# Feed-forward stage of an attention block: the second layer's first group of products ahead of the next block's projection

## The reference

```
y  = attention(x)                       # [4096, 1024]
x1 = layernorm(x + y @ Wproj)
h  = silu(x1 @ w1.T * s1) * (x1 @ w2.T * s2)      # layer one, 256 -> 1024
h  = gelu(h @ h1.T * s_h1)                        # layer two, 1024 -> 1024
h  = gelu(h @ h2.T * s_h2)                        # layer three
out = layernorm(x1 + h @ w3.T * s3)
```

## Time and profile before

| what | us |
|---|---|
| median of 3 runs | 3362.25 |
| lowest and highest run | 3346.83, 3367.85 |
| profiled execution, time | 3363.94 |
| profiled execution, span | 3362.1 |
| TensorE busy in the span | 3158.6 (94%) |
| mean granted clock of TensorE | 0.975 |

### The profile page before, as it was taken

One profiled execution on the slowest core, in us unless ns is written; L12 is line 12 of the kernel. 1 busy time (PEld: TensorE's weight loads), 2 busy tenths in 40 slices (PEclk: granted clock), 3 DMA queues, 4 the chain that ended last, 5 costly groups with the idle time before them and its releaser, 6 DMA issues. The chain is left out here.

```text
span 3362.1 us, 45968 instructions
## 1 busy us (share of the span) xinstructions
PE 3158.6 (94%) x15472; PEld 2462.0 (73%) x15472; DVE 1671.5 (50%) x3928; ACT 1792.8 (53%) x3057; POOL 1491.0 (44%) x1306
## 2 busy tenths in 40 slices
PE   3899999999999999999999999989999999999998
PEld 3667767667667677676676776678888888788887
DVE  6566566565565655665655656442222322232322
ACT  2477677676666766776766767742222222322222
POOL 4476676666665766766666666611111110000000
PEclk8899999999999999999999999989999999999999
DMA  2332332422432313324224225232222223111110
GB/s 74 69 86 47 84 72 47 93 62 60 95 71 67 88 44 85 68 50 93 62 60 95 62 58 147 60 120 87 86 88 86 86 85 116 65 47 67 47 67 19
DMA packets 196523, 249.12 MB, mean 74 GB/s; under 512 B 67264, under 2 KB 95040, under 8 KB 196160
## 3 DMA queue, kind: packets, MB, share of 16 engines
q1 hardware_dynamic: 196288, 246.19, 28.5%
HBM read 84.86 MB, written 43.52 MB: 38 GB/s over the span
## 5 line engine op out<-in xcount | busy, mean ns | idle before, releaser
L457 POOL TENSOR_TENSOR e_lo<-e_all,e_hi 128x512 fp32r<-128x512 f32 (+1 forms) x832 | 1034.1, 1251 | 661.4 <-ACT e_all L723 588.0
L723 ACT ACTIVATE e_all<-ps_s,bias 128x512 f32<-128x512 f32 (+3 forms) x1280 | 787.4, 622 | 168.6 <-PE ps_s L1030 82.2
L910 DVE TENSOR_REDUCE maxes<-ps_m 128x1 f32<-128x512 f32 x768 | 521.2, 686 | 374.2 <-PE ps_m L1008 371.5
L716 ACT ACTIVATE e_hi<-ps_s,bias 128x512 fp32r<-128x512 f32 (+1 forms) x832 | 559.1, 672 | 231.6 <-PE ps_s L1028 134.2
L1008 PE MATMUL ps_m<-k_ext,q_max 128*128 128x512 f32 (+3 forms) x1280 | 463.1, 383 | 55.6 <-DVE maxes L910 24.8
L1027 PE MATMUL ps_s<-q_twice,k_split 128*128 128x512 f32 (+3 forms) x1280 | 477.7, 373 | 30.2 <-ACT e_all L723 25.4
L1028 PE MATMUL ps_s<-q_ext,k_ext 128*128 128x512 f32 (+3 forms) x1280 | 471.2, 368 | 0.0
L1061 PE MATMUL ps_v<-e_lo,v_main 128*66 128x512 f32 (+1 forms) x832 | 433.6, 521 | 17.1 <-POOL e_lo L457 17.1
L1008 PEld LDWEIGHTS ps_m<-k_ext,q_max 128*128 128x128 f32 x1280 | 246.3, 193 | 205.8 <-issue 61.5
L907 DVE CUSTOM_DVE_ANT_0 ps_m<-ps_m,mask_row 128x128 f32<-128x128 f32 (+3 forms) x512 | 252.5, 496 | 284.0 <-PE ps_m L1008 283.8
L1045 PE MATMUL ps_v<-e_all,v_full 128*66 128x512 f32 (+2 forms) x896 | 324.9, 444 | 0.0
(11 more groups left out here) (245 smaller groups left out, 6127.4 us busy)
## 6 DMA issues: line engine op xcount, KB each, us to landing
q_twice<-q_max SPq DMA_DIRECT2D x256, 128.0 KB, 2.3
yt<-y_out SPq DMA_DIRECT2D x128, 130.0 KB
k_ext<-kq_hi SPq DMA_DIRECT2D x128, 128.0 KB, 2.3
q_max<-kq_hi SPq DMA_DIRECT2D x128, 128.0 KB, 2.4
k_split<-kq_hi SPq DMA_DIRECT2D x128, 128.0 KB, 2.4
k_split<-kq_lo SPq DMA_DIRECT2D x128, 128.0 KB, 2.4
q_ext<-kq_lo SPq DMA_DIRECT2D x128, 128.0 KB, 2.4
hidden<-gelu SPq DMA_DIRECT2D x64, 256.0 KB, 2.0
```

Source lines behind the costliest of these rows:

```text
L457: on.tensor_tensor(e_lo[:, i % LO_RING, off:QB], e_all[:, u_ % E_RING, off:QB], e_hi[:, i % HI_RING, off:QB].bitcast(F32), ALU.subtract).t ...
L716: nc.scalar.activation(e_hi[:, i % HI_RING, off:QB], ps_s[u_ % 2][:, off:QB], ACT.Exp, bias=by).then_inc(hi_done, 1)
L723: nc.scalar.activation(e_all[:, u_ % E_RING, off:QB], ps_s[u_ % 2][:, off:QB], ACT.Exp, bias=by).then_inc(ex_done, 1)
L910: nc.vector.tensor_reduce(maxes[:, qt, kc:kc + 1], ps_m[m % 2][:, 0:width], AX.X, ALU.max).then_inc(mx_free, 1)
```

## The change

On TensorE, the pairs of parts (0, 1), (2, 3), (4, 5) and (6, 7) of the next block's y stood ahead of the second layer's groups 0, 1, 2 and 3. They now stand ahead of groups 1, 2, 3 and 4. On ScalarE the splits of parts 0 and 1 stay in the first layer (o = 6 and 7), and the pairs (2, 3), (4, 5) and (6, 7), which stood ahead of gelu 0, 1 and 2, now stand ahead of gelu 1, 2 and 3. The turn of x stays ahead of group 6. The lists of VectorE, GpSimd and SP are unchanged.

```
@@ ScalarE @@
                 for o in range(OC):
-                    if more and o < 3:
-                        split_y(i + 1, 2 * o + 2)
-                        split_y(i + 1, 2 * o + 3)
+                    if more and 1 <= o < OC // 2:
+                        split_y(i + 1, 2 * o)
+                        split_y(i + 1, 2 * o + 1)
                     if o == TURN and more:
                         turn_x(i + 1)
@@ TensorE @@
                 for o in range(OC):
                     col = slice(o * P, (o + 1) * P)
-                    if o < OC // 2 and more:
-                        project_y(i + 1, 2 * o)
-                        project_y(i + 1, 2 * o + 1)
+                    if 1 <= o <= OC // 2 and more:
+                        project_y(i + 1, 2 * o - 2)
+                        project_y(i + 1, 2 * o - 1)
                     if o == TURN and more:
                         turn_x(i + 1)
```

## The result

The changed kernel takes 3318.2 us (median of 4 runs, 3314.34 to 3324.45), the kernel before 3359.7 in the same comparison. The ratio is 0.9882 with a 95% interval of 0.9846 to 0.9917, so between 28 and 52 us are gone; the forecast was 42.6 us and 3320. The profiled execution took 3318.82 us, of which 3317.0 are its span, 45.1 less than before.

A forecast was written before the change was run, and what follows sets the result against it. TensorE, busy 94% of the span, was taken as the bound, time being won only where it stands still or runs slowly. 7 x 6.25 - 1.1 = 42.6 us off 3362.25 gave 3320 us, range 3306 to 3339.

The forecast's parts named there:

- The two losses of a place, 3.72 and 2.53 us: Between the layers in seven blocks: TensorE stands 3.72 us, then low clock costs 2.53 us; 6.25 us each, all saved.
- Group 0 covered for 1.8 us: Group 0 straight after layer one: p_lo of group 7 ends 1.8 us before its product needs it; no cost.
- Parts 2 to 7 and SP's queue at no cost: Later splits, loads and stores: each ready before TensorE wants it, parts 2 and 3 by over 4 us; cost nothing.
- given back at the pairs: Rival at each pair: a late y_lo or load costs up to 1 us a block, 3327 us; chance 0.09.
- The turn of x, 5 us of cover: LayerNorm chain before the turn: takes 6.1 us, has two groups (11.1 us) instead of three; no cost, 5 us left.
- Block 0: At group 0 there, behind the wait for all weights: 1.1 us of the old wait stays, once; bounds 0.9 and 1.4.
- The clock rivals: At the joint of the layers: clock stays low or swings, only 3.72 us a block go, 3337 us; stays-low chance 0.09.
- the exchange of layers: Rival at the joint: this, not the stop, brings the clock down; 24.9 us saved, 3337 us; chance 0.09.
- The pattern in which small stops at each group make the clock swing: Mechanism from the Trainium skill: small stops between groups changing PSUM banks swing the clock; 3337 us, no separate chance.
- the chain as I gave it: Old joint: the projection waits for tail silu, prod, p_hi, p_lo, y_lo in turn; 3.72 us lost.

The follow-up runs named there:

- Experiment 1: Kernel before, with 15 useless products of 512 columns filling TensorE's stop between the layers in seven blocks: 3347.53 us, ratio 0.9957.
- Experiment 5: Changed kernel, but group 0 of layer two waits for all eight parts of p before its first product: 3358.15 us, ratio 0.9999.
- experiments 6 and 7: Changed kernel with the turn of x ahead of group 5 (6) or group 4 (7) on all engines: 3325.36 us and 3376.9 us.
- experiment 3: Kernel before with ScalarE's half of the change alone, TensorE keeping the old order: 3409.85 us, ratio 1.0142.
- experiment 4: Kernel before, with only VectorE's order changed, y_lo of part 0 right after p_lo of group 6: 3339.51 us, ratio 0.9934.

## Why the prediction was right

**The two losses of a place, 3.72 and 2.53 us.** Both held. The period fell by 6.24 us in the mean of six (37.4 / 6), against 6.25 worked out. Experiment 1 takes away the second alone and finds 2.41: the pair is 2.33 us shorter, and 0.1 at the group behind. Experiment 5 brings both back, in smaller sizes (3.2 and 1.9 us). That the median of 3318.2 came within 2 us of the forecast is luck, since medians scatter by more than that; the mechanism is borne out by the period.

**Group 0 covered for 1.8 us.** Right: its product with part 7 had 1.79 us in the joint shown. Experiment 5 shows that the part-by-part wait is what makes it so.

**Parts 2 to 7 and SP's queue at no cost.** Right for this profile: TensorE has no wait for `y_lo` in ffn_up. Nothing was given back at the pairs, so that rival is out.

**The turn of x, 5 us of cover.** Right; measured 5.0 in the profile, and experiments 6 and 7 show what the edge costs.

**Block 0.** The net was right (5.08 us against 5.15), the two terms in it were not. The place cost 6.4 us there before, not 6.25: its stop was 4.07 us, and the pair behind it took 5.20 instead of 2.84. And 1.3 us were left after the change, not 1.1: only 0.3 ahead of group 0, where I expected all of it, 0.1 in that group, and 0.9 in the group of layer one before, where the transposition of the last weights came late:

```profile
2233.97 1.29 POOL L1265 TENSOR_TENSOR y_in<-y_in,r_in 128x512 f32<-128x512 f32 x1 [31.43 <-DMA r_in<-recip_sums]
2234.21 1.61 DVE L1408 TENSOR_TENSOR p_lo<-prod,p_hi 128x512 fp32r<-128x512 f32 x1 [0.70 <-ACT p_hi L1314]
...
2236.57 1.23 PE L1437 MATMUL up_t<-ident,up_stage 128*128 128x128 f32 x8 [0.58 <-DVE h_lo L1355]
...
2240.73 0.51 PE L1492 MATMUL up_h<-p_hi,h_hi 128*128 128x512 f32 x1 [0.16 <-DVE h_lo L1355]
```

VectorE's `h_lo` stood behind a `p_lo` of 1.61 us beside a product of GpSimd, where the other `p_lo` of this block take 0.69. The prediction had held a `p_lo` this long to be harmless at group 0; it did not ask about the weights. Two small misses that cancel are luck, of 0.2 us.

**The clock rivals.** That the clock falls at the exchange of layers is refuted by the windows after and by experiment 1. The pattern in which small stops at each group make the clock swing did not appear either: over the three stops of 2.2 us a block of experiment 3 it stayed at 1.00.

**What I passed over.** ScalarE's half of the change was costed at nothing, rightly, but I did not ask whether it was needed: it was not. The bank that the projection shares with layer one was not in the chain as I gave it; it did not matter for this change, but it limits the other repair (experiment 4).

## What to carry to other kernels

Where a bound engine stops because its next task waits for the last link of a chain, look for later work whose inputs are mostly ready and can be waited for piece by piece, and put that in front; then read how long each piece moved behind it has until it is wanted. Cost a stop of TensorE as two terms, the time it stands and the slower products after it, and take the second from the profile's windows: here it was 40% of the loss. It is a reading of one place and not a constant: stops of 3.2 and 6.2 us cost 1.9 and 1.8 us more in the mean (experiments 5 and 7). When a change has halves on two engines, run each alone: here one was all of the gain, and the other alone was 48 us slower.

## What the runs showed of the hardware

The price of the low clock is not fixed. After the old stop of 3.7 us it was 2.4 to 2.5 us in the block examined. After the stop of 3.2 us of experiment 5, which is the same in every block (3.44 us from start to start, less 0.23), group 0 of blocks 1 to 6 took 6.93, 7.19, 8.35, 6.91, 7.19 and 8.36 us instead of 5.55: 1.4, 1.6, 2.8 us and the same three again. After the 6.2 us stop of experiment 7 the price went to and fro between 1.3 and 2.3 us (periods of 86.5 to 87.6 us, less 79.06 and 6.2), 1.8 in the mean. So a longer stop did not cost more, and the differences come in a fixed order, which scatter would not do; what sets the order is open. Stops of 1.8 and 2.2 us left the granted clock at 1.00 in experiments 4 and 3. What stops between 2.2 and 3.2 us do, no run shows.

The profile's periods repeat to a few hundredths of a microsecond (79.05 to 79.06 us in six blocks after the change), while the medians of the same kernels scatter by several microseconds. Here the small terms could be read from the periods alone.
